# Moving one batch's row selection into the other batch's first stage, with the two batches out of step

## The reference, cut to what matters

```
a = tanh(x @ WA.T);  b = x @ WB.T;  g = sigmoid(x @ Wg.T + bg);  dx = x @ WD.T + bD
h[t] = a[t] * h[t-1] + b[t]                      # 16 states, scan over 4096 tokens
x = layernorm(x + (h @ WC.T) * g + dx * (1 - g))
weights = x @ router_w + router_b;  k = 512
topv, topi = top_k(weights, k);  sel_idx = sort(topi[:, :k-1])
x_sel, pos_sel, w_sel = x[sel_idx], position_ids[sel_idx], weights[sel_idx]
m_sel = mask[sel_idx][:, sel_idx]                # rows, then columns, of a 1024 x 1024 mask
x1 = x_sel + attention(rmsnorm(x_sel), rope by pos_sel, m_sel)   # 16 heads of 16
x2 = x1 + gelu(rmsnorm(x1) @ w1) @ w2            # 256 -> 1024 -> 256
out[sel_idx] = x2 * w_sel;  all others keep x;  result = layernorm(x + out)
```

## Time and profile before

| | us |
|---|---|
| median of 3 runs | 534.05 (533.18 to 535.07) |
| the profiled execution | 536.87 |
| its span | 535.0 |
| busy PE / DVE / ACT / POOL | 449.4 / 391.9 / 291.8 / 173.5 |
| mean granted clock of PE | 0.926 of full |

### The profile page before, as it was taken

One profiled execution on the slowest core, in us unless ns is written; L12 is line 12 of the kernel. 1 busy time (PEld: TensorE's weight loads), 2 busy tenths in 40 slices (PEclk: granted clock), 3 DMA queues, 4 the chain that ended last, 5 costly groups with the idle time before them and its releaser, 6 DMA issues.

```text
span 535.0 us, 10439 instructions
## 1 busy us (share of the span) xinstructions
PE 449.4 (84%) x3410; PEld 334.2 (62%) x3410; DVE 391.9 (73%) x1216; ACT 291.8 (55%) x615; POOL 173.5 (32%) x210
## 2 busy tenths in 40 slices
PE   3699999898999342798879999998998999997970
PEld 2477888786887232666657666674785666663560
DVE  2687898798898688848379999938459999937050
ACT  2244646444655260016879999915678999932200
POOL 9146667676767620470241000001000000002232
PEclk9999999998999855579998999998999999997995
DMA  8613342342231210186620000000000000000100
GB/s 257 191 41 80 104 133 80 116 121 79 80 118 41 78 40 1 42 261 250 235 80 2 4 0 1 1 2 0 1 1 0 4 1 0 2 3 10 31 29 11
DMA packets 29846, 33.85 MB, mean 63 GB/s; under 512 B 6340, under 2 KB 25448, under 8 KB 29800
## 3 DMA queue, kind: packets, MB, share of 16 engines
q1 hardware_dynamic: 23024, 24.78, 14.4%
q0 software_dynamic: 3520, 8.40, 5.1%
q10 hardware_dynamic: 3256, 0.10, 0.4%
HBM read 19.63 MB, written 13.63 MB: 62 GB/s over the span
## 4 chain that ended last, share of the span: by engine, by line
PE 39%; DVE 13%; issue 12%; POOL 9%; ACT 5%; DMA 1%; POOLq 1%; DVEq 0%; ACTq 0%
PE ps L896 9%; PE ps L912 6%; PE ps L966 6%; PE ps L883 5%; PE ps L973 4%; POOL arena L489 3%; PE ps L833 3%; PE ps L852 2%; POOL r L498 2%; POOL h_parts L548 1%; PE ps L837 1%; PE ps L859 1%; POOL rq L503 1%; DVE arena L1380 1%; ACT arena L1174 1%
## 5 line engine op out<-in xcount | busy, mean ns | idle before, releaser
L1174 ACT ACTIVATE arena<-arena,nmax 128x511 f32<-128x511 f32 x128 | 92.0, 720 | 7.7 <-DVE nmax L1587 6.8
L1587 DVE CUSTOM_DVE_ANT_0 arena<-ps,nmask 128x511 f32<-128x511 f32 x128 | 84.7, 683 | 0.5 <-DVE nmask L1535 0.2
L896 PE MATMUL ps<-ident,arena 128*128 128x128 f32 x512 | 79.8, 279 | 3.7 <-DVE big L394 1.3
L896 PEld LDWEIGHTS ps<-ident,arena 128*128 128x128 f32 x512 | 60.5, 142 | 24.6 <-ACT arena L1174 15.0
L621 POOL COPY arena<-v_sb 128x256 f32<-128x256 f32 (+1 forms) x8 | 3.2, 399 | 152.2 <-PE ps L912 152.1
L680 PE MATMUL ps<-wgd_hi,x_hi 128*128 128x512 f32 x128 | 51.9, 405 | 0.0
L394 DVE COPY big<-ps 128x512 f32<-128x512 f32 x64 | 44.0, 688 | 9.8 <-PE ps L896 9.3
L883 PE MATMUL ps<-arena 96*128 (+1 forms) x128 | 49.1, 389 | 2.1 <-DVE nmask L1535 1.1
L681 PE MATMUL ps<-wgd_lo,x_hi 128*128 128x512 f32 x128 | 50.6, 395 | 0.0
L682 PE MATMUL ps<-wgd_hi,x_lo 128*128 128x512 f32 x128 | 50.6, 395 | 0.0
L489 POOL TENSOR_TENSOR arena<-arena 128x512 f32<-128x512 f32 x32 | 41.4, 1295 | 12.4 <-DVE arena L1280 10.8
(11 more groups left out here) (233 smaller groups left out, 978.4 us busy)
## 6 DMA issues: line engine op xcount, KB each, us to landing
arena<-in_L_attn_x SPq DMA_DIRECT2D x16, 512.0 KB, 4.6
out<-ob_sb SPq DMA_DIRECT2D x16, 512.0 KB, 3.2
w_sb<-in_L_ffn_w SPq DMA_DIRECT2D x2, 1024.0 KB, 10.5
mt_scratch<-nmask SPq DMA_DIRECT2D x8, 256.0 KB, 2.7
mt_scratch<-big SPq DMA_DIRECT2D x8, 256.0 KB, 3.1
big<-in_L_attn_Wg SPq DMA_DIRECT2D x1, 256.0 KB, 4.2
big<-in_L_attn_WD SPq DMA_DIRECT2D x1, 256.0 KB, 4.9
wqk<-in_L_ffn_wq SPq DMA_DIRECT2D x1, 256.0 KB, 7.8
```

The lines of the kernel that those rows point to most:

```text
L896: mm = pe.transpose(ps[:, 2 + u % 2, k * P:(k + 1) * P], pr[u % 4][:, k * P:(k + 1) * P], ident[:, :])
L1174: act.activation(pr[u % 4][:, 0:K - 1], sm[u % 4][:, 0:K - 1], ACT.Exp, bias=nmax[:, c, h:h + 1], scale=-1.0, accum_out=rsum[:, c, h:h + 1 ...
L1587: dve.tensor_tensor_reduce(sm[u % 4][:, 0:K - 1], ps[:, S_BANKS[u % AHEAD], 0:K - 1], nmask[b][:, c, 0:K - 1], 1.0, 3.4e38, ALU.add, ALU.m ...
```

## The change

The order of each engine's program is written by hand, and the change rewrites it. Line numbers of the changed kernel are larger by 7 to 50.

- The search of batch 0 stands inside the first stage. DVE has one round after `products(G - 1, 1)` and one after `products(G, 0)` in the iterations `G` = 10 to 13; `mark` and `slots` are in 14, `at_hi` and `lo_vals` (now two functions) in 15, `rows` and `factors` in 16, ahead of the last group's second statistics. PE has the counts between its transposes.
- The router's row is read from SBUF, and the aggregates go to SBUF, since bank 1 now holds batch 0's counts.
- POOL gathers batch 0's rows in the last iteration, after `total(15, 1)` and ahead of `scales(15)`; the mask's rows follow. `normalise(15)` on ACT waits for `scales(15)`, and the scaling of the weights still stands behind it.
- The search of batch 1, its slots and one-hots stand between rope and split of batch 0 in the preparation. Copies of v move from DVE to ACT.
- Batch 1's row gather and its mask rows are issued in the attention of batch 0 (POOL); turning its mask rows, first norm and all four projections stand in the middle, ahead of `hidden(0)`.
- The scratch of the mask is written by blocks of four columns' quarters: the same 16 transfers of 256 KB, in pieces of 512 bytes in place of 2048, so that one gathered row block can be turned before the next has landed.

```diff
             for G in range(NGB + 1):
                 if G > 0:
                     products(G - 1, 1)
+                    if NG + 2 <= G < NG + 6:
+                        if G > NG + 2:
+                            narrow(0, 2 * (G - NG) - 5)
+                        compare(0, 2 * (G - NG) - 4)
+                    if G == NG + 6:
+                        narrow(0, 7)
+                        mark(0)
+                    if G == NG + 7:
+                        one_hot_hi(0)
+                    if G == NGB:
+                        rows(0)
                     half_statistics(G - 1, 0)
+                    if G == NGB:
+                        factors(0)
...
                 if G < NGB:
                     products(G, 0)
+                if NG + 2 <= G < NG + 6:
+                    narrow(0, 2 * (G - NG) - 4)
+                    compare(0, 2 * (G - NG) - 3)
+                if G == NG + 6:
+                    slots(0)
+                if G == NG + 7:
+                    one_hot_lo(0)
...
-                    step.done(dve.tensor_tensor_reduce(junk[:, t, :], s_sb[j][:, t, :], ps[:, 1, 0:D], 1.0, 0.0,
+                    step.done(dve.tensor_tensor_reduce(junk[:, t, :], s_sb[j][:, t, :], rw_row[:, :], 1.0, 0.0,
...
                 if 0 <= G - 1:
                     total(G - 1, 1)
+                    if G == NGB:
+                        pool.wait_ge(rows_ready[0], 3)
+                        for j in range(2):
+                            pool.wait_ge(out_stored[j], 16 * NG // 2)
+                        gather_x(0)
                     scales(G - 1)
...
+            gather_mask_rows(0)
             factors(1)
             split_values(1)
...
+                turned = mt_dram[b].rearrange("(h n s) (c q) -> c h s n q", h=2, s=P, c=C)
...
+            logits(1)
+            compare(1, 0)
+            cosines(0)
+            narrow(1, 0)
+            compare(1, 1)
+            rope(0, 0)
...
+            mark(1)
+            copy_turned(0, 1)
+            parts(0, 3)
+            slots(1)
+            copy_turned(0, 2)
+            one_hot_hi(1)
+            one_hot_lo(1)
+            copy_turned(0, 3)
             rows(1)
+            copy_mask()
+            factors(1)
+            angles(1)
+
+            attention(0)
```

More of the change, by code:

```diff
@@ new lines, in _ @@
+            turn_mask_block(0, 0)
+            count(1, 4)
+            turn_mask_block(0, 1)
+            count(1, 5)
+            turn_split(0, 0)
+            turn_mask_block(0, 2)
+            count(1, 6)
+            turn_mask_block(0, 3)
+            count(1, 7)
+            turn_split(0, 1)
+            flag_sums(1)
+            turn_split(0, 2)
+            turn_split(0, 3)
+            pick_rows(1)
+            for c in range(C):
+                turn_mask_columns(0, c)
+            pick_rest(1)
@@ L1019, in _ @@
+            attention(1)
+            pe.wait_ge(onT_ready, B * TURNS)
+            for c in range(C):
+                project_out(1, c, range(TURNS - 1, TURNS))
+            turn_hn(1)
+            hidden(1)
+            for c in range(C):
+                second_product(1, c)
         @block.scalar
@@ L1243, in _ @@
+            hidden(0)
+            more_parts(1, 0)
+            for c in range(1, C):
+                more_parts(1, c)
+                copy_turned(1, c - 1)
+                copy_second_mask(c - 1)
+            copy_turned(1, C - 1)
+            copy_second_mask(C - 1)
+            attention(1)
+            copy_hnT(1)
+            hidden(1)
         @block.vector
@@ L1449, in factors @@
                 step.link(dve.tensor_scalar(keep_m[:, b, :], picked[:, b, :, ABOVE], -1.0, 2.0, ALU.mult, ALU.add))
-            logits(1)
-            for r in range(ROUNDS):
-                for b in range(B):
-                    if r:
-                        narrow(b, r - 1)
-                    compare(b, r)
-            for b in range(B):
-                narrow(b, ROUNDS - 1)
-            for b in range(B):
-                mark(b)
-            slots(0)
-            one_hots(0)
-            slots(1)
@@ new lines, in _ @@
+            for c in range(KD):
+                dve.wait_ge(wt_copied, c + 2)
+                dve.tensor_tensor(wgd_lo[:, c, :], ps[:, 3 + c, :], wgd_hi[:, c, :].bitcast(F32),
+                                  ALU.subtract).then_inc(split_ready, 1)
+            rest_of_x(1, 0)
+            scan(0)
+            step.link(dve.tensor_reduce(is_lo[:, 0:1], ident[0:HROWS, N:2 * N], X, ALU.add))
+            step.done(dve.tensor_scalar(is_lo[:, 1:2], is_lo[:, 0:1], -1.0, 1.0, ALU.mult, ALU.add))
+            step.link(dve.tensor_tensor(wc_lo[:, :], ps[0:HROWS, 5, 0:D], wc_hi[:, :].bitcast(F32), ALU.subtract))
@@ new lines, in _ @@
+            copy_turned(0, 0)
+            narrow(1, 6)
+            compare(1, 7)
+            parts(0, 2)
+            narrow(1, 7)
+            mark(1)
+            copy_turned(0, 1)
+            parts(0, 3)
[4 more added lines that the diff above has]
+            copy_turned(0, 3)
+            rows(1)
+            copy_mask()
+            factors(1)
+            angles(1)
+            attention(0)
+            for c in range(C):
+                first_normalised(1, c)
```

614 lines of the change are left out of this document (303 added, 311 removed).

## The result

| | after |
|---|---|
| median of 4 runs | 547.96 us (545.5 to 549.13); the kernel before beside it 534.43 |
| ratio | 1.025 (95% interval 1.0206 to 1.0294) |
| profiled execution / its span | 548.9 / 547.2 us |
| busy PE / DVE / ACT / POOL | 455.7 / 404.5 / 295.0 / 176.8 us |

551 was forecast. The span grew by 12.2 us, and it splits at the same events as the forecast did: the first gather came 13.1 us earlier (219.23 to 206.11), the preparation is 13.4 longer, the first attention 0.6 shorter, the middle 12.1 longer and the rest 0.5 longer. A second pair of traces of the same two kernels (`before_again` and `after_again`) gives 14.1 earlier, then 15.3, 0.0, 11.3 and 0.2, together 12.7 us. A part is thus known to 1 or 2 us, the whole better.

A forecast was written before the change was run, and what follows sets the result against it. PE was busy throughout a first-stage group, DVE and a POOL-DVE loop close behind. A -10.6, B +13.8 and C +14.0 sum to +17.2, from the 534.05 us median to 551; own range 540 to 562, 8 in 10 535 to 570.

The forecast's parts named there:

- A: First stage: shift of the first gather, from 219.23 to 208.6 us, -10.6; bounds -28 and +4.
- C: Middle between the attentions: mask tiles, norm, four projections and column turns added, +14.0 us; bounds +12 and +16.
- B: Preparation, first gather to first scores: 72 us against 58.2, +13.8; bounds +8 and +22.
- V: End of L1305 of group 14 in the first stage: moves by 23.8 us, from 177.8 to 201.6.
- the dots: First stage: dot products with two SBUF inputs meet POOL's sums, 0.5 us in about ten groups, 5.0; bounds 0 and 10.
- the collisions of the rounds: First stage: the round after `products(G - 1, 1)` waits for POOL, 2.7 us beyond cover; iterations 11 to 13 cost 3.2 each.
- rival 2: First stage: POOL's powers block DVE too, four groups' second rounds held 3 us more, `slots` too: +12, median 563; chance 0.14.
- The rule that was weighed: Two-SBUF-input DVE instructions contend with SBUF-reading POOL ones; the first issued holds the shared pair throughout, so powers would block rounds.
- The `at_hi` of iteration 15: First stage: 2.29 us, waits up to 1.3 for POOL, then holds up `total(14, 1)` and the statistics: 5.0 us.
- Rival 1: First stage takes the search for nothing: V stays at 177.8, gather at 184.8, median 527 us; chance 0.10.
- Rival 3: First stage: no collisions but full work, gather at 191.3, 535 us, no change to speak of; chance 0.14.
- The mark of 11 us: Sign in the first stage: groups of iterations 11 to 13 under 11 us show rival 3, 12 to 13 the forecast.

The follow-up runs named there:

- the three together: Changed kernel with search rounds moved off POOL's sums, all dots from PSUM, weights scaled early and `normalise(15)` behind the sines: 525.27 us, 0.9848 of the kernel before.
- `a_order`: Changed kernel with both search rounds of an iteration where POOL runs no sum, behind the statistics and behind the scan; dots still read SBUF: 544.0 us.
- the probe in SBUF against PSUM: Kernel before plus five dependent 32-column additions in iterations 3 to 15, both inputs in SBUF or one in PSUM: 1.0562 and 1.0151 of the kernel before.

## Why the prediction was right, point by point

The direction and the three terms were right; some sizes within the terms, and which instructions are hit, were not. That the time came out so near (551 for 548) is in part luck. Of the change itself 17.2 us were forecast, and 12.2 and 12.7 measured in the two pairs of traces (13.5 and 13.2 between the medians). A and C were both set 2 to 3.5 us too high, and inside A and B errors of both signs cancel.

**A, forecast -10.6, measured -13.1.** V was to move by 23.8 and moved by 21.8. Step by step, from the shift of each `rq`: iteration 10, 1.2 forecast and 0.8 measured; 11 to 13, 9.6 and 8.7 (2.3, 2.8, 3.6); 14, 3.0 and 1.7; 15, 5.0 and 4.9; the dots up to there, 5.0 and 5.8, of which 1.6 lay already in the first `rq`, where an unchanged kernel varies by as much (37.5 and 39.95 in two runs of the changed one). From V to the gather 6.4 for 7.0.
- The experiments split it otherwise. From the first `rq` to that of group 14 the kernel before takes 139.6 us, the three together 147.6, `a_order` 154.3, and the changed kernel 159.8 and 161.0. So the search's own work is some 8.0 us (forecast 6.5), the dots 6.7 (forecast 5.0), and what the order of the rounds adds, their collisions above all, 5.5 to 6.7, where the forecast had 12.3 (23.8 less 6.5 less 5.0). The term that was sized worst is the collisions of the rounds: one instruction of 0.2 us held for 1.15 in most groups, not two held over 2.7 us. The 3.2 us for an iteration do not even come out of the terms as worded (2.7 + 0.6 + 0.4 is 3.7; 3.2 needs the whole 1.1 us of idle time taken off 2.7 + 1.2 + 0.4).
- That the one round collides and the other doesn't was right, and rival 2 is refuted: in `a_order` a round stands beside `rq`, `nb` and `r` and takes what it takes alone. The rule that was weighed (the Trainium skill, SBUF — State Buffer, Who interferes with whom) would have held it there; the earlier trace rows was the better guide.
- Which instructions would be stretched, I had wrong. I named L1381 and L1374 at over 1 us. L1381 took 0.51 at most and L1374 0.41. It was mostly what comes between them, L1384 or L1386, whichever was next when the sum began, at 1.15 to 1.17. L1384 is a `tensor_scalar` in bfloat16 with one tensor in SBUF as its input, which I had not counted among those that could be; L1410 of `slots`, another, took 1.31. The Trainium skill (SBUF — State Buffer, Who interferes with whom) says that `tensor_scalar` in a two-port mode takes the shared ports too. The trace agrees in that L1384 is held (1.16 against 0.23); in which mode it ran, no trace shows.
- The dots are the term that I set too low. 0.5 a group was near (0.6 measured), but I gave it to ten groups; alone it costs 9 us over fifteen. It is also the part of A that bought nothing: the counts and the row fit in one bank, as the kernel with all three parts shows.
- The `at_hi` of iteration 15 did one of the two things forecast: it waited for nothing (2.28 us, as alone), and POOL's sum beside it took 3.16.

**B, forecast +13.8, measured +13.4 (15.3 in the second pair).** The first projection was to start 16.7 us behind the gather and did at 15.2, for the reason given; 1.2 of the difference is that the four gathers took 5.0 us in place of 6.2 (the first one 1.22, where it had been 2.36). The rest was to last 55.3 and lasted 56.3. In it PE was back at full clock with the second projection (1.88 us at 226.64), so that DVE waited 3.2 us for the first three counts and not 6.0. From the sines on it waited 9.7 in all, where the forecast had 10.4 and 0.7, and worked for 44.8, where it had 42.3. The term that carries B is ACT's order: undone, it gives back 9.0 of the 13.4 in the same windows (its two halves, the scalings and the normalisation, were not tried apart). The forecast had put 9.7 ahead of the first projection and 4.1 behind it, and 8.1 and 5.2 were measured. The 4.4 us that are left are what the whole search, slots and one-hots of batch 1 cost here, less what has left the preparation (batch 1's projections, its first norm, the copies of v on DVE); these two were not measured apart. The mask's smaller pieces cost nothing on this path, as forecast: PE turned the gathered columns (L813, at 267.80) straight behind the picks, without a wait.

**C, forecast +14.0, measured +12.1 (11.3 in the second pair).** The terms listed for the time ahead of `hidden` add up to 376.7 and not to 377.5, so +13.2 is what they give. `hidden` starts 19.6 us behind the last `project_out` (20 forecast), 11.6 later than before. Behind it the sixteen column turns were to add 1.9 and the stretch grew by 0.5 (37.09 for 36.56). The turns did cost 1.8, but the forecast had left out PE's clock. In the kernel before, `turn_hn` ran at half clock behind a wait of 2.27 us, and `hidden` was not at full clock throughout. Windows of that kernel, with the columns of the earlier trace rows:

```profile
363.50:365.44 1.94, 1.94 (x8) 1.48 (x9) 1.87 (x7) 0.59 (x1) 0.00 (x0) 0.50 0.00 0
365.44:380.00 14.56, 14.56 (x34) 6.58 (x34) 11.71 (x29) 6.05 (x9) 0.00 (x0) 0.95 0.00 0
```

Now projections stand ahead of them, the granted clock is 1.00 throughout, and `hidden` takes 13.98 us in place of 14.65. Tiles of mask rows took 3.66 us of PE under ACT's copies (4.03 forecast). POOL's gathers for batch 1 cost nothing, as forecast: the first attention is 0.6 us shorter.

**The rivals.** Rival 1 (search for nothing) needed the gather before 191.4; it came at 206.1. Rival 3 (no collisions) needed groups under 11 us; they took 12.3 to 13.3, and the probe in SBUF against PSUM shows the collision by itself. The mark of 11 us was set a little low: where collisions are taken away, in the three together, these groups still take 11.1 to 11.7 us, and the gather is at 194.1, near the 191.3 that it gave.

## What to carry to other kernels

Work moved into "idle" time of DVE is to be laid against what POOL does at that moment, and a try costs little: ask of each inserted instruction whether both inputs are in SBUF (or whether it is a `tensor_scalar` like L1384), and put it beside POOL's powers or its waits, not beside its long sums. When a stage is taken apart, look at the in-order queues that it had kept busy: here the dearest term that could be undone (9.0 us of the preparation) was nine harmless scalings on ACT and one normalisation, which the moved gather had put on the critical path. A tensor that was moved to make room (the router's row) is part of the price of the change; try it alone first.

## What the runs showed of the hardware

- Five dependent additions of 128 x 32 took 2.3 us on average (1.15 to 3.04) with both inputs in SBUF and 1.08 us with one in PSUM, in the same place beside POOL's `rest_of_h` and sum of 512 columns.
- POOL's powers of 4 and 8 columns (1.01 and 1.64 us) held up no DVE instruction in any trace here: 0.19 and 0.41 us beside them, as alone.
- A dot product of 256 columns with both inputs in SBUF took 0.41 us alone, and 1.13 to 1.52 when it was issued in the first 0.4 us of POOL's sum, ending some 0.3 us behind it; the reverse, DVE first, took POOL's sum from 1.3 to 3.16 us under a DVE instruction of 2.28.
- One wait of 1.9 us, after ten at full clock, was followed by 4.3 us in which PE was granted 0.61 of it, a mixture of 2.4 and 1.2 GHz; one of 2.27 us in the kernel before by 1.9 us at 0.50.
- The kernel before took 534 us in three sets and 543 to 549 in all 17 runs of another, while the three together took 525 in both of theirs; the cause is open.
